# A longer assumed delay between dependent steps in the list scheduler of a fused graph convolution and expert network, while edge tiles are left

## The chip, the core and the metric

One core of a Trainium2 chip runs the kernel as one program. It has five instruction queues that run each in their own order and meet only at semaphores: TensorE (PE), VectorE (DVE), ScalarE (ACT), GpSimd (POOL) and SyncE (SP, which here only issues DMAs). The metric is the device time of the program in microseconds (us), lower is better.

## What is computed

Cut to what matters (6,250 nodes, 106,250 edges, width 256; 8 experts of hidden width 1,024, the best two per node):

```python
z   = layernorm(x) @ W * norm_src                  # per node
h   = segment_sum(z[src], dst) * norm_dst + b      # gather by edge, sum by target node
x   = x + relu(h)
n   = layernorm(x)
top_p, top_idx = top_k(softmax(layernorm(n) @ Wr + br), 2)
y_e = gelu(xe @ W1[e] + b1[e]) @ W2[e] + b2[e]     # for the two experts of each node
out = x + sum(weights * y_e)
```

The layer norm of the second network has a gain and a shift per expert, and W is applied behind the sum.

## The kernel before

**Edges.** The edges, sorted by target, are cut in 832 edge tiles of 128 edges. For each tile POOL gathers 128 rows of the table `zt` with one indirect DMA (L830) into one of 23 buffers `gt` (a gather waits until the tile 22 places earlier has been used), and PE multiplies them by a 0/1 matrix `S` (L1159, step `tile`). Eight tiles make a run, which DVE adds to the sums in `acc` (L1528, step `add`).

**Node tiles.** The 49 tiles of 128 nodes lie in 15 groups and 8 chunks. As soon as the edges of a group are summed, each node tile runs through the steps `nT` (PE transposes, ACT copies), `nW` (product with W on PE), `hh` (DVE: relu, residual, statistics), `xT` (transpose again) and `lg` (router logits on PE). `nd1` and `nd2` are DVE work per group ahead and behind. When a chunk is whole, `r1`, `r3`, `r5`, `r6` compute the routing, and POOL sends its rows by expert to DRAM (`xs`, L858, two indirect DMAs for each node tile: a **send**).

**Blocks.** A block is 256 rows of one expert; there are 56, and a chunk's blocks can start when its rows are sent. SP loads the rows and weights (`ld`: rows `xb` L1018, `w1b` L1022; `ld2`: `w2b` L1028, bias L1032). Then `turn` (PE transposes L1229, ACT copies), `low` (DVE, L1650, the lower halves `xe`), four `up` steps (PE, 12 products each, L1245; ACT computes the gelu L1106 and a copy L1110), a `split` on DVE behind each (L1656), two `down` steps (PE, 24 products each, L1260) and `y` on DVE (L1682). The loads of `w1b` for block m wait until the four `up` of block m-2 are done.

**Results.** Blocks 0 to 33 hold rows of the chunks 0 to 5. Their results are stored to a table `ys` in DRAM by SP (`st`, L985). When all edge tiles and all of these stores are done, POOL **fetches them back** for the 41 node tiles of these chunks (`cg`, L877, two DMAs each); DVE adds the two rows of each node with their weights (`cc`, L1695 and L1696), and four sums (`sums`, L899) add the outcome to `out`. The blocks 34 to 55 add theirs to `out` by an indirect DMA with addition, two for each block (a **give**, L890). Gives and sums form one chain: each waits until the one ahead of it has landed. Four of these 22 blocks are of chunk 6, and 18 (38 to 55) of chunk 7, the last, whose sends need the last edge tile.

**Order.** A scheduler, `plan()`, writes one list of steps in Python when the program is built, and each engine takes its own part of that list in the list's order. `plan()` keeps a clock of its own for each engine, and lets a step be listed when what it depends on is done by that clock. The end of a step, as its dependents see it, is what `emit` returns: the costs, and `HAND` = 0.5 on top.

Of the kernel before, what the change touches and what calls it, by code (L numbers as in the profile page):

```python
# [159 lines left out]
PARTS = {"wa": ("w", "wb"), "wc": ("w", "wd"), "we": ("w", "wf"), "nW": ("n", "hh"), "r3": ("r", "r5")}  # L160


ROUTE = {f"r{i}": i for i in range(10)}


def plan():
# [4 lines left out]
    later, sent = [], {}  # L171

    turns, used = [], set()
    HAND, SLACK = 0.5, 0.5

    BEHIND = [1.25 * min(8, (R * CT - 1 - i) // 2) for i in range(R * CT)]

    def emit(kind, arg, costs, ready):
        order.append((kind, arg))
        t = ready  # L180
        for eng, us in costs:
            t = max(t, clock[eng]) + us
            clock[eng] = t
            t += 0.2
        return t + HAND

    def free(costs):
        return all(clock[eng] <= s["now"] + (3.0 if i else 1.0) for i, (eng, _) in enumerate(costs) if eng != "POOL")
# [1 line left out]
    def due():  # L190

        done = False
        while later and later[0][0] <= s["now"]:
            at, kind, arg, costs, then = later.pop(0)
            end = emit(kind, arg, costs, at)
            then(end)
            done = True
        return done
# [6 lines left out]
    def blocks():  # L205
# [12 lines left out]
        def turn(m):  # L218
            end = emit("turn", m, (("PE", 0.55), ("ACT", 0.65)), s["now"])
            after(end, "low", m, (("DVE", 0.75),), lambda e: low.__setitem__(m, e))  # L220

        def up(m, q):
            end = emit("up", (m, q), (("PE", 1.35), ("ACT", 1.85)), s["now"])
            after(end, "split", (m, q), (("DVE", 0.8),), lambda e: split.__setitem__((m, q), e))
# [183 lines left out]
    n = R * CT  # L408
    at = {"g": 0, "fetch": 0, "tile": 0}
# [46 lines left out]
def gnn_ffn(nc, x, src, dst, W, b, Wr, br, ln_g, ln_b, W1, b1, W2, b2, out):  # L456
# [3 lines left out]
    ACT = mybir.ActivationFunctionType  # L460
    X = mybir.AxisListType.X
    ORDER = plan()

    ctx = ExitStack()
    with ctx:
# [798 lines left out]
        def vector(e):  # L1264
            made = {"n": 0}

            def then(inst):

                made["n"] += 1
                inst.then_inc(s_chain, 1)  # L1270
                e.wait_ge(s_chain, made["n"])
# [242 lines left out]
            for kind, arg in ORDER:  # L1514
# [112 lines left out]
                elif kind == "lr":  # L1627
# [7 lines left out]
                    then(e.tensor_tensor(lg[:, js, :], lg[:, js, :], br_bc[:, :].unsqueeze(1).to_broadcast([128, n, E]), ALU.add))  # L1635
                elif kind in ROUTE:
                    route(arg, ROUTE[kind])
                elif kind == "turn":
# [88 lines left out]
```

## Time and profile before

| | us |
|---|---|
| median of 3 runs | 1662.88 |
| lowest and highest | 1661.35, 1666.77 |
| span of the profiled execution | 1657.8 |
| PE busy | 1196.1 |
| POOL busy | 1122.3 |
| DVE busy | 951.9 |
| ACT busy | 595.5 |

The median of the runs is 5.1 us above the profiled execution's span; this much is taken for what lies around the span. The trace knows three stages. Up to about 160 us the tables are made. Then the gathers run, up to about 1336 us, with node tiles and blocks in between. Behind them lies the end stage, with the last chunk, the fetches back, the last blocks and the gives. In a row of a timeline the first number is the start from the start of the span, the second the duration, and the bracket the idle time ahead of it on its engine with what ended it.

### The profile page before, as it was taken

The numbers are of one execution on the slowest core, as the hardware profiler recorded it, in microseconds if no ns is written. First come the engines' busy times: TensorE is split into PE (matmuls) and PEld (weight loads), VectorE is DVE, ScalarE is ACT, GpSimd is POOL, SyncE is SP. The second block draws the span as 40 slices with busy tenths as digits, with TensorE's granted clock in tenths as the row PEclk, the third lists the DMA queues.
The fourth block names the chain that finished last, engine by engine and source line by source line (L and its number), as shares of the span: only waits on it lengthen the run. The fifth ranks groups of instructions, "written<-read, shape, count | busy, mean of one in ns | idle before, by whom it ended". The sixth has DMA issues, their size and how long they took to land.

```text
span 1657.8 us, 26613 instructions
## 1 busy us (share of the span) xinstructions
PE 1196.1 (72%) x9098; PEld 988.4 (60%) x9098; DVE 951.9 (57%) x2502; ACT 595.5 (36%) x1169; POOL 1122.3 (68%) x1116
## 2 busy tenths in 40 slices
PE   6954556756358555995499649969848868688996
PEld 5954344535147224983388439848728746577995
DVE  8997457556435252657264744764645639465543
ACT  4954011111032003540345125515315335355663
POOL 5006777777777777777777777777777757864333
PEclk9999566557579557996799769979959969899998
DMA  6027866776485348974787569869659578999983
GB/s 187 1 97 264 270 218 214 220 230 180 129 261 163 110 117 262 293 241 130 251 283 246 144 202 320 272 193 300 188 185 307 171 239 240 279 305 289 255 243 93
DMA packets 262266, 356.06 MB, mean 215 GB/s; under 512 B 25476, under 2 KB 225702, under 8 KB 262132
## 3 DMA queue, kind: packets, MB, share of 16 engines
q1 hardware_dynamic: 195544, 205.39, 38.4%
q0 software_dynamic: 60224, 142.57, 30.1%
q10 hardware_dynamic: 6364, 6.40, 1.2%
q8 instruction: 73, 1.20, 0.3%
q14 instruction: 61, 0.50, 0.1%
HBM read 290.80 MB, written 65.38 MB: 215 GB/s over the span
## 4 chain that ended last, share of the span: by engine, by line
PE 36%; DMA 23%; POOL 18%; issue 9%; DVE 9%; ACT 3%; SPq 1%; POOLq 0%; DVEq 0%; ACTq 0%
DMA gt<-zt,srcI 12%; PE ps L1245 9%; PE ps L1260 9%; POOL gt L830 9%; PE ps L1159 8%; POOL xs L858 5%; DMA out<-gt,toks 4%; PE ps L1134 2%; PE ps L1170 2%; DVE ohl L1334 2%; PE ps L1197 2%; POOL out L890 2%; ACT h L1106 2%; POOL S L877 1%; DMA out<-acc 1%
## 5 line engine op out<-in xcount | busy, mean ns | idle before, releaser
L830 POOL DMA_INDIRECT gt<-zt,srcI x832 | 832.8, 1001 | 254.2 <-issue 180.1
L1159 PE MATMUL ps<-gt,S 128*128 128x257 f16 x1664 | 346.9, 332 | 199.6 <-DMA gt<-zt,srcI 198.4
L1159 PEld LDWEIGHTS ps<-gt,S 128*128 128x128 f16 x1664 | 202.9, 152 | 298.9 <-DMA gt<-zt,srcI 283.2
L1245 PE MATMUL ps<-xe,w1b 128*128 128x256 f16 x2688 | 345.5, 283 | 40.7 <-DVE xe L1650 19.9
L1260 PE MATMUL ps<-w2b,hT 128*128 128x256 f16 x2688 | 313.3, 274 | 13.4 <-DVE yb L1682 6.8
L1245 PEld LDWEIGHTS ps<-xe,w1b 128*128 128x128 f16 x2688 | 270.3, 101 | 85.3 <-DVE xe L1650 22.6
L1106 ACT ACTIVATE h<-ps,cb 128x256 f32<-128x256 f32 x448 | 227.5, 558 | 251.4 <-PE ps L1245 250.2
L1656 DVE SCALAR_TENSOR_TENSOR hT<-h,cb,hT 128x512 f16<-128x512 f32 x224 | 167.5, 749 | 235.1 <-ACT hT L1110 234.5
L1260 PEld LDWEIGHTS ps<-w2b,hT 128*128 128x128 f16 x2688 | 263.4, 98 | 46.9 <-issue 12.8
L1110 ACT ACTIVATE hT<-h,cb 128x512 f16<-128x512 f32 x224 | 161.7, 722 | 7.3
L1084 ACT ACTIVATE aT<-ps 128x256 f32<-128x256 f32 x98 | 37.5, 382 | 316.4 <-PE ps L1190 316.3
L1382 DVE TENSOR_TENSOR S<-dlo,S 128x1024 f16<-128x1024 f16 x104 | 71.7, 690 | 103.1 <-PE ps L1159 102.4
L890 POOL DMA_INDIRECT out<-gt,toks x38 | 63.0, 1657 | 94.6 <-DMA out<-gt,toks 52.7
L858 POOL DMA_INDIRECT xs<-xrow,slI x98 | 98.4, 1004 | 31.9 <-issue 29.6
L1094 ACT ACTIVATE xe<-ps 128x512 f16<-128x512 f32 x56 | 32.5, 580 | 238.6 <-PE ps L1229 238.6
L1229 PE MATMUL ps<-ident,xb 128*128 128x128 f32 x224 | 37.8, 296 | 102.1 <-DMA xb<-xs 102.1
L1650 DVE SCALAR_TENSOR_TENSOR xe<-ps,xe 128x512 f16<-128x512 f32 x56 | 38.3, 683 | 118.0 <-ACT xe L1094 118.0
L1528 DVE SCALAR_TENSOR_TENSOR acc<-ps,dhi,acc 128x257 f32 x208 | 91.1, 479 | 22.9 <-PE ps L1159 10.6
L1229 PEld LDWEIGHTS ps<-ident,xb 128*128 128x128 f32 x224 | 28.3, 152 | 105.6 <-DMA xb<-xs 104.8
L1134 PE MATMUL ps<-ohh,ohl 128*128 128x49 bf16 x832 | 84.1, 278 | 9.8 <-DVE ohh L1335 9.2
L1134 PEld LDWEIGHTS ps<-ohh,ohl 128*128 128x128 bf16 x832 | 81.2, 150 | 12.9 <-DVE ohh L1335 12.9
L1170 PE MATMUL ps<-gb,w1b 128*128 128x1 f32 x256 | 51.9, 337 | 34.4 <-DMA w1b<-in_L_ffn_W 34.4
(261 smaller groups left out, 1253.0 us busy)
## 6 DMA issues: line engine op xcount, KB each, us to landing
w1b<-ws SPq DMA_DIRECT2D x56, 1024.0 KB, 6.6
w2b<-ws SPq DMA_DIRECT2D x56, 1024.0 KB, 9.2
ws<-w2b SPq DMA_DIRECT2D x16, 1024.0 KB, 5.3
xb<-xs SPq DMA_DIRECT2D x56, 260.0 KB, 8.0
gt<-zt,srcI POOLq DMA_INDIRECT x832, 3.8
ys<-yb SPq DMA_DIRECT2D x34, 256.0 KB, 7.4
w1b<-in_L_ffn_W SPq DMA_DIRECT2D x8, 1024.0 KB, 9.2
hT<-in_L_ffn_W SPq DMA_DIRECT2D x8, 1024.0 KB, 13.6
```

The lines of the kernel that those rows point to most:

```text
L830: e.indirect_dma_start(out=gt[:, i % NG, :], out_offset=None, in_=zt, in_offset=bass.IndirectOffsetOnAxis(ap=srcI[:, c, r:r + 1].bitcast(u ...
L858: e.indirect_dma_start(out=xs, out_offset=bass.IndirectOffsetOnAxis(ap=slI[:, i, CHUNKS[c][0] + j:CHUNKS[c][0] + j + 1].bitcast(u32), axis=0),
L890: e.indirect_dma_start(out=out, out_offset=bass.IndirectOffsetOnAxis(ap=toks[:, a, i:i + 1].bitcast(u32), axis=0), in_=late_rows(a)[:, i, ...
L1106: inst = e.activation(h32[n % NH][:, z, :], UP[n % 2][:, z * BS:(z + 1) * BS], ACT.Gelu, bias=cb[m % 3][:, 2 * q + z:2 * q + z + 1], scale ...
L1110: e.activation(hT[m % 2][:, 0, 2 * q:2 * q + 2, :], h32[n % NH][:, :, :], ACT.Copy, scale=cb[m % 3][:, 9:10]).then_inc(s_hi, 1)
L1134: inst = e.matmul(PS[6][:, 0:T], ohl[c % 2][:, :, j], ohh[c % 2][:, :, j], start=(c == 0 and j == 0), stop=(c == NCH - 1 and j == TC - 1))
L1159: inst = e.matmul(PS[r % 2][:, 0:257], S[:, r % NS, :, c], gt[:, i % NG, part * 257:part * 257 + 257], start=(c == 0 and part == 0), stop= ...
L1170: inst = e.matmul(PV[:, j:j + 1], w3[:, kk, j * 128:(j + 1) * 128], gb[:, ex, 2 + kk:3 + kk], start=(kk == 0), stop=(kk == 1))
L1245: inst = e.matmul(UP[n % 2][:, z * BS:(z + 1) * BS], w[:, l, kk, j * 128:(j + 1) * 128], xe[m % 2][:, k, kk, :], start=(kk == 0 and l == 0 ...
L1260: inst = e.matmul(PY[:, h * D:(h + 1) * D], hT[m % 2][:, k, j, h * 128:(h + 1) * 128], w[:, l, j, :], start=(j == 0 and l == 0 and k == 0) ...
L1528: inst = e.scalar_tensor_tensor(out=a, in0=PS[r % 2][:, 0:257], scalar=dhi[:, w, r:r + 1], in1=a, op0=ALU.mult, op1=ALU.add)
L1656: e.scalar_tensor_tensor(out=hT[m % 2][:, 1, 2 * q:2 * q + 2, :], in0=h32[n % NH][:, :, :], scalar=cb[m % 3][:, 9:10], in1=hT[m % 2][:, 0, ...
```

## The change

`emit` adds 2.5 in place of 0.5 behind the steps `turn`, `low`, `up`, `split`, `down`, `nT`, `nW`, `hh` and `xT`, as long as the list has not yet come to the last edge tile (`at["tile"] < n`, n = 832). No instruction is added or taken away (3,360 steps in both lists); the steps change their places.

```diff
@@ -160,6 +160,9 @@
+SPREAD = ("turn", "low", "up", "split", "down", "nT", "nW", "hh", "xT")
@@ -171,7 +174,7 @@
-    HAND, SLACK = 0.5, 0.5
+    HAND, SLACK, FAR_HAND = 0.5, 0.5, 2.5
@@ -182,7 +185,7 @@
-        return t + HAND
+        return t + (FAR_HAND if kind in SPREAD and at["tile"] < n else HAND)
```

In the list of before, the `y` of block 30 stands behind edge tile 785, that of block 33 behind tile 824, and block 34 is the next when the edge tiles end. In the list of the change the `y` of block 30 stands behind tile 813, and behind the last edge tile come the last `up` of block 32, half of block 31's `down`, all of block 32's, and the whole of block 33 from its first `up` on. Lines behind the new constants are three higher.

**First place: the end of the gathers.** On PE, from the last edge tile on: L1190 and L1193 are the transposes of node tiles, L1197 and L1200 the product with W, L1206 and L1209 the logits, L1245 and L1248 `up`, L1260 and L1263 `down`, L1229 and L1232 `turn`. Before:

```order
L1159 MATMUL ps<-gt,S 128x257 x8
L1190 MATMUL ps<-ident,acc 128x128 x4
L1245 MATMUL ps<-xe,w1b 128x256 x12
L1197 MATMUL ps<-W_sb,aT 128x256 x2
L1190 MATMUL ps<-ident,acc 128x128 x2
L1245 MATMUL ps<-xe,w1b 128x256 x24
L1229 MATMUL ps<-ident,xb 128x128 x4
L1197 MATMUL ps<-W_sb,aT 128x256 x2
L1190 MATMUL ps<-ident,acc 128x128 x2
L1245 MATMUL ps<-xe,w1b 128x256 x12
L1206 MATMUL ps<-Wrc,aT 128x8 x2
L1197 MATMUL ps<-W_sb,aT 128x256 x2
```

With the change:

```order
L1162 MATMUL ps<-gt,S 128x257 x2
L1193 MATMUL ps<-ident,acc 128x128 x4
L1248 MATMUL ps<-xe,w1b 128x256 x12
L1263 MATMUL ps<-w2b,hT 128x256 x24
L1200 MATMUL ps<-W_sb,aT 128x256 x2
L1193 MATMUL ps<-ident,acc 128x128 x2
L1248 MATMUL ps<-xe,w1b 128x256 x24
L1200 MATMUL ps<-W_sb,aT 128x256 x2
L1193 MATMUL ps<-ident,acc 128x128 x2
L1263 MATMUL ps<-w2b,hT 128x256 x24
L1209 MATMUL ps<-Wrc,aT 128x8 x2
L1248 MATMUL ps<-xe,w1b 128x256 x24
```

Before, the first products are those of block 34; now those of the blocks 32, 31 and 33 stand ahead of it, and `down` steps lie between the steps of the node tiles.

On POOL, at the same place: L830 and L833 are gathers, L858 and L861 sends (8 DMAs for chunk 6, then 8 for chunk 7), L877 and L880 fetches back, L890 and L893 gives, L899 and L902 the first sum. Before:

```order
L830 DMA gt<-zt,srcI 128x514 x71
L858 DMA xs<-xrow,slI 53504x260 x8
L830 DMA gt<-zt,srcI 128x514 x7
L877 DMA S<-ys,cidx 128x256 x8
L877 DMA gt<-ys,cidx 128x256 x6
L877 DMA xrow<-ys,cidx 128x256 x6
L877 DMA S<-ys,cidx 128x256 x6
L890 DMA out<-yb,toks 6250x256 x2
L877 DMA S<-ys,cidx 128x256 x2
L877 DMA gt<-ys,cidx 128x256 x4
L899 DMA out<-acc 128x10x256
L858 DMA xs<-xrow,slI 53504x260 x8
```

With the change:

```order
L833 DMA gt<-zt,srcI 128x514 x68
L861 DMA xs<-xrow,slI 53504x260 x8
L880 DMA S<-ys,cidx 128x256 x8
L880 DMA gt<-ys,cidx 128x256 x6
L861 DMA xs<-xrow,slI 53504x260 x8
L893 DMA out<-yb,toks 6250x256 x2
L880 DMA xrow<-ys,cidx 128x256 x6
L880 DMA S<-ys,cidx 128x256 x4
L893 DMA out<-yb,toks 6250x256 x2
L880 DMA S<-ys,cidx 128x256 x4
L880 DMA gt<-ys,cidx 128x256 x2
```

The sends of chunk 6 moved behind the last gather. The sends of chunk 7 moved ahead of the first give and of most fetches back: 14 fetch DMAs stand ahead of them, and 32 did before.

**Second place: SP around the store of block 33** (with buffer numbers; L985 and L988 are the store `ys<-yb0`, L1018 and L1021 a block's rows, L1022 and L1025 its `w1b`). Before:

```order
L1032 DMA b2b0<-in_L0_ffn_b2 128x256
L1018 ISA
L1018 DMA xb3<-xs 128x2x260
L1022 ISA
L1022 DMA w1b1<-ws0 128x8x512
L985 DMA ys<-yb0 128x2x256
L938 DMA xin<-in_x 106x256
```

With the change:

```order
L948 TENSOR_LOAD ek6
L948 ISA x2
L1021 ISA
L1021 DMA xb0<-xs 128x2x260
L1025 ISA
L1025 DMA w1b0<-ws0 128x8x512
L988 DMA ys<-yb0 128x2x256
L1031 DMA w2b1<-ws1 128x8x512
```

Before, the store stands behind `w1b1` of block 35; now behind `w1b0` of block 36.

**Third place: DVE at the first block of chunk 7.** L1646 and L1649 are the DVE part of `turn` of block 38, L1650 and L1653 its `low`, L1695 to L1699 `cc`, with the buffer that the fetched rows lie in. Before:

```order
L1695 TENSOR_SCALAR acc<-gt,wts 128x256
L1696 SCALAR_TENSOR_TENSOR acc<-gt,wts,acc 128x256
L1642 TENSOR_LOAD ek
L1642 ISA x2
L1646 ISA
L1646 COPY cb<-cbt 128x12
L1695 TENSOR_SCALAR acc<-xrow,wts 128x256
L1696 SCALAR_TENSOR_TENSOR acc<-xrow,wts,acc 128x256
L1650 SCALAR_TENSOR_TENSOR xe<-ps,xe 128x512
```

With the change:

```order
L1698 TENSOR_SCALAR acc<-S,wts 128x256
L1699 SCALAR_TENSOR_TENSOR acc<-S,wts,acc 128x256
L1645 TENSOR_LOAD ek
L1645 ISA x2
L1649 ISA
L1649 COPY cb<-cbt 128x12
L1698 TENSOR_SCALAR acc<-S,wts 128x256
L1699 SCALAR_TENSOR_TENSOR acc<-S,wts,acc 128x256
L1698 TENSOR_SCALAR acc<-gt,wts 128x256
L1699 SCALAR_TENSOR_TENSOR acc<-gt,wts,acc 128x256
L1653 SCALAR_TENSOR_TENSOR xe<-ps,xe 128x512
```

Ahead of this `low` stood the `cc` of node tile 17 with that of 16 ahead of it; now it is those of the tiles 12, 13 and 14, which the new list of POOL fetches behind the sends of chunk 7 and behind two gives.

## Rows read from the trace of the kernel before

**Rows 1.** The profile's page: span, busy time and share of each engine.

```profile
span 1657.8 us, 26613 instructions
...
PE 1196.1 (72%) x9098; PEld 988.4 (60%) x9098; DVE 951.9 (57%) x2502; ACT 595.5 (36%) x1169; POOL 1122.3 (68%) x1116
```

**Rows 2.** Waits of POOL, 161 to 1338 us: releaser: us in total, times, longest.

```profile
POOL gt L830 <- issue: 173.4, 569, 0.3
POOL gt L830 <- PE ps L1159: 73.7, 242, 0.3
POOL xs L858 <- issue: 27.4, 90, 0.3
```

**Rows 3.** Waits of PE, 400 to 1340 us, same columns.

```profile
PE ps L1229 <- DMA xb<-xs: 98.2, 7, 28.1
...
PE ps L1190 <- ACT aT L1084: 11.2, 15, 1.6
```

**Rows 4.** Timeline of POOL: start, us, operation [idle before it <-releaser].

```profile
1317.89 1.02 POOL L858 DMA_INDIRECT xs<-xrow,slI  x1 [0.30 <-issue]
...
1328.27 0.99 POOL L830 DMA_INDIRECT gt<-zt,srcI  x1 [0.30 <-issue]
...
1335.83 0.95 POOL L830 DMA_INDIRECT gt<-zt,srcI  x1 [0.30 <-issue]
1347.60 0.94 POOL L877 DMA_INDIRECT S<-ys,cidx  x1 [10.81 <-DMA ys<-yb]
1348.85 0.94 POOL L877 DMA_INDIRECT S<-ys,cidx  x1 [0.30 <-issue]
```

**Rows 5.** Timeline of PE, same columns: last edge tile, blocks 37, 38 and 55.

```profile
1342.59 0.65 PE L1159 MATMUL ps<-gt,S 128*128 128x257 f16 x2 [1.10 <-DMA gt<-zt,srcI]
...
1397.47 2.78 PE L1245 MATMUL ps<-xe,w1b 128*128 128x256 f16 x24
1400.09 2.78 PE L1260 MATMUL ps<-w2b,hT 128*128 128x256 f16 x24
...
1423.74 6.66 PE L1245 MATMUL ps<-xe,w1b 128*128 128x256 f16 x36 [3.51 <-DVE xe L1650]
...
1639.63 5.40 PE L1260 MATMUL ps<-w2b,hT 128*128 128x256 f16 x48 [1.70 <-DVE gt L1682]
```

**Rows 6.** Timeline of SP's DMA issues; then issues by line, us to landing last.

```profile
1334.47 3.81 SPq L985 DMA_DIRECT2D ys<-yb  x1
...
ys<-yb SPq DMA_DIRECT2D x34, 256.0 KB, 7.4
```

**Rows 7.** Timeline of DVE: last node tile, its group, a fetched row.

```profile
1372.75 0.18 DVE L1605 BATCH_NORM_AGGREGATE mv<-st 128x2 f32<-128x6 f32 x1
...
1375.59 0.17 DVE L1281 SCALAR_TENSOR_TENSOR ra<-tm,ra 128x8 f32<-128x8 f32 x1
...
1422.21 0.35 DVE L1695 TENSOR_SCALAR acc<-xrow,wts 128x256 f32<-128x256 f32 x1 [4.16 <-DMA xrow<-ys,cidx]
```

**Rows 8.** Timeline of POOL after the edges: a send, fetches back, gives.

```profile
1397.60 1.07 POOL L858 DMA_INDIRECT xs<-xrow,slI  x1 [2.30 <-DVE slI L1445]
...
1408.27 1.59 POOL L890 DMA_INDIRECT out<-yb,toks  x1 [0.30 <-issue]
...
1412.05 1.04 POOL L877 DMA_INDIRECT gt<-ys,cidx  x1 [0.30 <-DVE acc L1696]
...
1415.93 0.95 POOL L877 DMA_INDIRECT xrow<-ys,cidx  x1 [0.30 <-DMA out<-yb,toks]
...
1546.90 1.66 POOL L890 DMA_INDIRECT out<-gt,toks  x1 [12.14 <-DMA out<-acc]
...
1636.95 1.55 POOL L890 DMA_INDIRECT out<-gt,toks  x1 [7.69 <-DMA out<-gt,toks]
...
1647.83 1.55 POOL L890 DMA_INDIRECT out<-gt,toks  x1 [2.06 <-DMA out<-gt,toks]
```

**Rows 9.** Waits of PE, 1424 to 1646 us, columns as in Rows 2.

```profile
PE ps L1245 <- DVE xe L1650: 14.5, 6, 3.5
```

## The prediction

> **What bounds the kernel now.** I read the page first: in a span of 1657.8 us PE is busy for 1196.1 and POOL for 1122.3 [rows 1], and no engine is full. Such shares hide that the program has two stages with different limits, so I ask each stage which wait ends last.
>
> *While gathers run* (161 to 1338 us): the waits of POOL [rows 2] show that no gather and no send waited longer than 0.3 us. The 0.3 us is the normal step between two DMAs, so POOL issues one about each 1.25 to 1.3 us from first to last, and its own issue sets the pace. PE waits for the gathers, and much for the first rows of a chunk: 98.2 us in 7 waits, the longest 28.1 [rows 3]. Even behind that one POOL did not wait, since 23 buffers lie between them. The waits of PE for other engines' results, which the change wants to lessen, are small: the largest kind is 11.2 us, for ACT's copies [rows 3]. Nothing that PE saves here can pull a gather forward.
>
> *Behind the gathers*: the last gather starts at 1335.83, the last edge tile ends at 1342.59 + 0.65 = 1343.24 [rows 4, 5]. POOL then waits 10.8 us for the store of block 33 and starts the fetches back at 1347.60 [rows 4]. From there it works almost without a gap, and then from give to give: 1546.90 to 1636.95 are 10 gives, 9.0 us each, each held by the landing of the one ahead; the last two come 5.4 us apart [rows 8], when PE has ended or nearly so and loads no more weights. PE runs the 18 blocks of chunk 7 from 1423.74 and ends at about 1645 [rows 5]; the last give starts at 1647.83 [rows 8]. So two chains end together. The one of POOL has been behind its inputs since the sums, and I take it as the bound: what delays the first fetch back, delays the end.
>
> **The change part by part.** Up to the last gather the counts are the same, and POOL sets the pace, so the new places cost nothing there; the cover is the 23 buffers, and it would be gone if PE fell 22 tiles behind (27 us at 1.25).
>
> *Sends of chunk 6 behind the last gather.* Eight DMAs of (1328.27 - 1317.89) / 8 = 1.30 us leave the path of the gathers [rows 4]: the last gather starts at 1325.4, the last edge tile ends at 1343.2 - 10.4 = 1332.8. A gain of 10.4 for all that hangs on that tile.
>
> *Blocks pushed behind the last edge tile.* By the order of PE these are one quarter of the `up` of block 32, half of block 31's `down`, all of 32's, and block 33 whole. In units of 24 products of 2.62 us (1400.09 - 1397.47 [rows 5]): 0.5 + 1 + 2 + 4 = 7.5 units, 19.7 us of PE.
>
> *When block 33 is stored.* Its `y` now follows, on DVE, the statistics of the last node tile and the end of that group. Before, these statistics ended at 1372.93, 29.7 us behind the last edge tile, and the group's end took 2.8 more [rows 7]. PE has 6.5 units in that stretch where it had 4; I assume they fit, and price it at 2.5 x 2.62 = 6.5 us if not. So `y` ends at 1332.8 + 29.7 + 2.8 + 0.8 = 1366. Its store stands on SP behind the weights of block 36, which wait for the four `up` of block 34, and PE comes to these only behind block 33: 1362 for the last `down`, then 2 units with the node steps in between and a `turn`: 1369 to 1371. I take 1371. The store landed in 7.4 us at the median and in about 13 the last time (1334.47 to 1347.60 [rows 4, 6]), then behind much more queued weight data; I take 10. The fetches back start at **1381**, 33.4 us later than before. Bounds: 1369 + 7.4 = 1376 (+29), and 1371 + 6.5 + 13 = 1391 (+43).
>
> The Trainium skill ("DMA: Bandwidth & Descriptors", section "Anatomy of one DMA — SWDGE (gpsimd) path") gives about 2.0 us fixed plus bytes over 436 GB/s: as an estimate 2.6 us for these 256 KB, and the sum would be 7.4 us less by it. It states this for GpSimd's DMAs, this one is SP's, and the row of 7.4 speaks against it; the row decides.
>
> *From the first fetch back to the gives.* 82 fetches, 8 sends, 9 gives and 4 sums stand there in both orders, so I keep before's distance to the give at 1546.90, less the 2.3 us that POOL waited for the slots of chunk 7 [rows 8], which are now known before POOL asks. So this give starts at 1546.9 + 33.4 - 2.3 = 1578.
>
> *When chunk 7's blocks start.* Its sends now stand behind 14 fetches, but the `low` of block 38 stands on DVE behind the `cc` of node tile 14. Ahead of that tile's second row lie 29 fetches of 1.25 (1348.85 - 1347.60 [rows 4]), 8 sends of 1.3 and two gives of 3.8 (1412.05 - 1408.27 [rows 8]): 1381 + 36.3 + 10.4 + 7.6 = 1435.3. The fetch that held this `low` before was issued at 1415.93 [rows 8], and DVE took it up at 1422.21 after a wait of 4.16 [rows 7]: 6.3 us. With `cc` and `low`, 1.5 us, `up` starts at 1443 instead of 1423.74: PE is 19 us later, POOL's chain 31.
>
> *Sum.* PE ends 12 us earlier against the chain than before, so 12 / 9.0 = 1.3 gives more run at 5.4 and not at 9.0: -4.8. 33.4 - 2.3 - 4.8 = **+26.3 us**, span 1684.1. With the 5.1 us by which the median stands above the span: **1689 us**. Bounds: 29 - 2.3 - 4.8 = +22 and 43 - 2.3 - 4.8 = +36; half a microsecond more or less for each of 10 gives adds 5 at both ends: 1680 to 1704.
>
> **Rivals.** *PE alone sets the end.* If the gives catch up on the late fetches (POOL is idle for over half of each 9 us), only PE's work counts: 19.7 more, 10.4 earlier, +9.3 at most, and less where the work falls in PE's idle time there: 1663 to 1672. For it: PE and gives end within 3 us of each other. Against: each give waited for the one ahead, long after its own block was done, and `cc` 14 holds PE too.
>
> *Faster: chunk 7 sets the end.* Its path starts at the last edge tile, which comes 10.4 us earlier; if all behind it moves along, 1662.9 - 10.4 = 1652.5. For it: the 10.4 us are sure. It decides at the fetches: the sends were at 1397.60 [rows 8] and would have to be at 1387.2, so the 14 fetches (17.8 us) would have to start by 1369.4, where I have 1381 and 1376 at the earliest.
>
> The rule of the Trainium skill that speaks for a gain is "Perfetto Trace Analysis", section "Optimization Strategies": keep the matmul engine as busy as possible and unblock what it waits for. By it the waits of 11.2 us in [rows 3] would come off the end; that POOL never waited says they would not.
>
> *More: DVE's order makes every block wait.* If each of the ten blocks up to the last `cc` waits 3.5 us for fetched rows, the longest such wait now, PE gets 35 us where 14.5 of the kind are in its present run [rows 9]: its end is 1645 + 19 + 20.5 = 1684.5, and with the 12.8 us from there to the span's end 1697.3: time 1702. It decides when PE ends after about 1679.
>
> *Nothing*: the list changes nothing that binds. The order of POOL and SP speaks against it; it is in the lower end of the PE rival.
>
> **Chances.** The forecast 0.67; PE alone 0.14 (half of it within 0.3% of now); faster 0.06; every block waits 0.11; none of these 0.02. A measurement of this kernel can tell about 0.3%, 5 us, from no change. Faster 0.07, same 0.07, slower 0.86. The range takes in the bounds of the sum and most of both rivals at its sides: 1672 to 1706.
>
> **What would show it.** Right: the last gather starts near 1325 with no wait of POOL above 0.3 us ahead of it; then POOL idle for 30 to 45 us until a store `ys<-yb`; the first `up` of block 38 near 1443 behind a DVE wait for fetched rows; gives about 9 us apart, the last four or so 5.4. Wrong: POOL waits for PE among the gathers; fetches back that start before 1370; gives held by DVE's `y` and not by the one ahead, which would be PE's bound; a node chain of over 36 us behind the last edge tile.

## The result, and the profile after

| | before | after |
|---|---|---|
| median, us | 1663.66 (4 runs) | 1683.45 (4 runs) |
| lowest and highest, us | 1661.35, 1666.77 | 1679.6, 1685.85 |
| span of the profiled execution, us | 1657.8 | 1684.4 |

The change makes the kernel slower: the ratio after to before is 1.0126, with a 95% interval of 1.0094 to 1.0157. The forecast was 1689, with a range from 1672 to 1706.

The page of the kernel after, first part, answers to [rows 1]. The share of PE even rises by a point while the time gets longer:

```profile
span 1684.4 us, 26608 instructions
...
PE 1224.4 (73%) x9098; PEld 1011.4 (60%) x9098; DVE 948.6 (56%) x2502; ACT 596.5 (35%) x1169; POOL 1125.2 (67%) x1116
```

**While gathers run.** Waits of POOL from 161 to 1325 us (releaser: us in total, times, longest), beside [rows 2]:

```profile
POOL gt L833 <- issue: 178.8, 587, 0.3
POOL gt L833 <- PE ps L1162: 66.7, 219, 0.3
POOL xs L861 <- issue: 25.0, 82, 0.3
```

As before, no gather waited longer than 0.3 us. And the waits of PE in this stage (400 to 1330 us), beside [rows 3]:

```profile
PE ps L1162 <- DMA gt<-zt,srcI: 151.0, 165, 3.8
PE ps L1232 <- DMA xb<-xs: 71.1, 4, 23.7
...
PE ps L1193 <- ACT aT L1087: 9.9, 16, 1.9
```

The wait for ACT's copies, which room between dependent steps should lessen, went from 11.2 to 9.9 us. The wait for the rows of chunks fell by 27 us, from 98.2 to 71.1, and that for the gathers rose by 33.5, from 117.5 to 151.0: what PE saves at one it waits at the other.

**Behind the gathers.** Timeline of POOL, beside [rows 4, 8]: the last gather, the first and last send of chunk 6, the first fetch back, the first send of chunk 7, the first give, the give behind the last sum, the last.

```profile
1328.72 1.07 POOL L833 DMA_INDIRECT gt<-zt,srcI  x1 [0.30 <-PE ps L1162]
1331.49 1.02 POOL L861 DMA_INDIRECT xs<-xrow,slI  x1 [1.70 <-DVE slI L1448]
...
1340.56 0.98 POOL L861 DMA_INDIRECT xs<-xrow,slI  x1 [0.30 <-issue]
1381.14 0.99 POOL L880 DMA_INDIRECT S<-ys,cidx  x1 [39.59 <-DMA ys<-yb]
...
1399.10 1.02 POOL L861 DMA_INDIRECT xs<-xrow,slI  x1 [0.30 <-issue]
...
1410.61 1.61 POOL L893 DMA_INDIRECT out<-yb,toks  x1 [0.30 <-issue]
...
1581.77 1.67 POOL L893 DMA_INDIRECT out<-gt,toks  x1 [15.27 <-DMA out<-acc]
...
1674.25 1.56 POOL L893 DMA_INDIRECT out<-gt,toks  x1 [2.06 <-DMA out<-gt,toks]
```

The one large new thing is the idle time of 39.6 us ahead of the first fetch back, where 10.8 stood. Everything behind it on POOL moved with it: the first fetch back by 33.5 us, the give behind the last sum by 34.9, the last give by 26.4, the span by 26.6.

The timeline of SP shows what the fetch waited for, beside [rows 6]: rows and weights of block 36, then the store of block 33, which stands behind them in the list.

```profile
1368.53 0.39 SPq L1021 DMA_DIRECT2D xb<-xs  x1
1373.62 0.39 SPq L1025 DMA_DIRECT2D w1b<-ws  x1
1374.06 0.58 SPq L988 DMA_DIRECT2D ys<-yb  x1
```

DVE, beside [rows 7]: the statistics of the last node tile, then `y` of block 33, ready 5.3 us before its store is issued. Those 5.3 us are a queue's order, and no work.

```profile
1365.11 0.18 DVE L1608 BATCH_NORM_AGGREGATE mv<-st 128x2 f32<-128x6 f32 x1
...
1367.97 0.75 DVE L1685 SCALAR_TENSOR_TENSOR yb<-ps,cb,b2b 128x512 f32<-128x512 f32 x1
```

PE, beside [rows 5]: the last edge tile, the first `up` of block 38, the last `down`.

```profile
1334.01 0.64 PE L1162 MATMUL ps<-gt,S 128*128 128x257 f16 x2
...
1446.75 4.22 PE L1248 MATMUL ps<-xe,w1b 128*128 128x256 f16 x36 [2.41 <-DVE xe L1653]
...
1651.90 5.40 PE L1263 MATMUL ps<-w2b,hT 128*128 128x256 f16 x48 [1.72 <-DVE gt L1685]
```

PE ends at 1657.3, 17 us ahead of the last give; before, it was 2.8 us.

### The profile page after: what moved, and what is told of

It is laid out like the page before. It is cut to its first block, busy times and chain, and to the rows that moved or that the text cites. A ratio compares the mean times of both kernels' runs of the same rounds, so it can differ in the third digit from the quotient of the medians.

```text
span 1684.4 us, 26608 instructions
## 1 busy us (share of the span) xinstructions
PE 1224.4 (73%) x9098; PEld 1011.4 (60%) x9098; DVE 948.6 (56%) x2502; ACT 596.5 (35%) x1169; POOL 1125.2 (67%) x1116
## 4 chain that ended last, share of the span: by engine, by line
PE 32%; DMA 29%; POOL 21%; issue 10%; DVE 7%; ACT 1%; POOLq 0%; DVEq 0%; SPq 0%; ACTq 0%
DMA gt<-zt,srcI 20%; POOL gt L833 11%; PE ps L1162 8%; PE ps L1263 8%; PE ps L1248 8%; POOL xs L861 5%; DMA out<-gt,toks 4%; PE ps L1137 2%; PE ps L1173 2%; DVE ohl L1337 2%; DMA out<-acc 2%; POOL out L893 2%; PE ps L1200 2%; DVE zh L1351 1%; POOL S L880 1%
## 5 line engine op out<-in xcount | busy, mean ns | idle before, releaser
L833 POOL DMA_INDIRECT gt<-zt,srcI x832 | 834.5, 1003 | 254.1 <-issue 185.8
L1248 PE MATMUL ps<-xe,w1b 128*128 128x256 f16 x2688 | 353.4, 287 | 17.6 <-DVE xe L1653 15.0
L1263 PE MATMUL ps<-w2b,hT 128*128 128x256 f16 x2688 | 323.2, 279 | 17.7 <-DVE yb L1685 13.8
L1248 PEld LDWEIGHTS ps<-xe,w1b 128*128 128x128 f16 x2688 | 276.3, 103 | 62.8 <-DVE xe L1653 19.0
L1263 PEld LDWEIGHTS ps<-w2b,hT 128*128 128x128 f16 x2688 | 268.5, 100 | 55.7 <-issue 17.6
L861 POOL DMA_INDIRECT xs<-xrow,slI x98 | 100.9, 1029 | 31.3 <-issue 29.6
L893 POOL DMA_INDIRECT out<-gt,toks x38 | 60.4, 1589 | 86.4 <-DMA out<-gt,toks 43.1
L1531 DVE SCALAR_TENSOR_TENSOR acc<-ps,dhi,acc 128x257 f32 x208 | 91.0, 479 | 29.1 <-PE ps L1162 12.2
L1232 PE MATMUL ps<-ident,xb 128*128 128x128 f32 x224 | 36.9, 291 | 71.1 <-DMA xb<-xs 71.1
L1173 PEld LDWEIGHTS ps<-gb,w1b 128*128 128x128 f32 x256 | 53.2, 321 | 34.7 <-issue 34.5
L1232 PEld LDWEIGHTS ps<-ident,xb 128*128 128x128 f32 x224 | 28.3, 151 | 72.8 <-DMA xb<-xs 72.0
```

The costliest lines, as they stand in the source:

```text
L833: e.indirect_dma_start(out=gt[:, i % NG, :], out_offset=None, in_=zt, in_offset=bass.IndirectOffsetOnAxis(ap=srcI[:, c, r:r + 1].bitcast(u ...
L861: e.indirect_dma_start(out=xs, out_offset=bass.IndirectOffsetOnAxis(ap=slI[:, i, CHUNKS[c][0] + j:CHUNKS[c][0] + j + 1].bitcast(u32), axis=0),
L893: e.indirect_dma_start(out=out, out_offset=bass.IndirectOffsetOnAxis(ap=toks[:, a, i:i + 1].bitcast(u32), axis=0), in_=late_rows(a)[:, i, ...
L1173: inst = e.matmul(PV[:, j:j + 1], w3[:, kk, j * 128:(j + 1) * 128], gb[:, ex, 2 + kk:3 + kk], start=(kk == 0), stop=(kk == 1))
L1248: inst = e.matmul(UP[n % 2][:, z * BS:(z + 1) * BS], w[:, l, kk, j * 128:(j + 1) * 128], xe[m % 2][:, k, kk, :], start=(kk == 0 and l == 0 ...
L1263: inst = e.matmul(PY[:, h * D:(h + 1) * D], hT[m % 2][:, k, j, h * 128:(h + 1) * 128], w[:, l, j, :], start=(j == 0 and l == 0 and k == 0) ...
```

## The experiments

In what follows "first fetch" is the start of the first fetch back, "last give" the start of the first DMA of the last block's give. In every kernel the span ends about 10 us after that start. The executions behind a profile vary by some us around their median, so the medians decide and the profile tells the place.

### On which stretch does it hang: spreading up to the end, or at the end alone

Theory A: the cost comes from what is pushed behind the last edge tile, so nearly all of it from the last 130 edge tiles. Its rival: the new order costs (or gains) within the gathers. Four kernels test it, each an edit of the kernel after. e1 ends the spreading 130 tiles before the end:

```diff
-        return t + (FAR_HAND if kind in SPREAD and at["tile"] < n else HAND)
+        return t + (FAR_HAND if kind in SPREAD and at["tile"] < n - 130 else HAND)
```

e2 spreads only there:

```diff
-        return t + (FAR_HAND if kind in SPREAD and at["tile"] < n else HAND)
+        return t + (FAR_HAND if kind in SPREAD and n - 130 <= at["tile"] < n else HAND)
```

e3 spreads only the steps of blocks, e4 only those of node tiles:

```diff
-SPREAD = ("turn", "low", "up", "split", "down", "nT", "nW", "hh", "xT")
+SPREAD = ("turn", "low", "up", "split", "down")
```

```diff
-SPREAD = ("turn", "low", "up", "split", "down", "nT", "nW", "hh", "xT")
+SPREAD = ("nT", "nW", "hh", "xT")
```

Expected of e1:

> The change, with the longer assumed delay given up once edge tile 702 is listed, 130 ahead of the end. Theory (the late fetches back carry the loss): block 33's result is listed ahead of the last edge tile again, its store is not behind the weights of block 36, the first fetch back starts at 1345 to 1352, and the time is that of the kernel before, 1658 to 1668. Rival (spreading costs through the gather stage itself): most of the stage is still spread, so at least half of the loss stays, 1673 or more.

Expected of e2:

> The reverse: the longer assumed delay is used only from edge tile 702 to the last. Three of the ten block steps behind the last edge tile are gone against the full change (all of block 33's down, half of its up and half of block 32's down twice remain), and the store stands ahead of block 36's weights. Theory: the first fetch back starts between 1360 and 1374, 7 to 20 us ahead of the full change, and the time is 1668 to 1678, between the two kernels. Rival (the spread of the gather stage costs): 1658 to 1667, as before the change.

Expected of e3:

> The longer delay for the steps of blocks alone (turn, low, up, split, down). Three down steps of the blocks 32 and 33 stand behind the last edge tile, the sends of chunk 6 are back among the gathers, so the last edge tile is 10 us later than with the full change. Theory: the first fetch back at 1363 to 1373, time 1669 to 1678. If PE's added work alone counted: 3 x 2.6 = 8 us of work, time 1664 to 1671.

Expected of e4:

> The longer delay for the steps of node tiles alone (nT, nW, hh, xT). The same three down steps stand behind the last edge tile, but the sends of chunk 6 come behind the last gather, which ends 10 us earlier. Theory: the first fetch back at 1353 to 1365, time 1661 to 1671. If PE's added work alone counted: 8 us of work less the 10 us head start, time 1657 to 1664.

Beside these four the kernel before itself took 1900.08 us (1888.6 to 1913.8), 14% more than in every other measurement of this document. Why is not known: the record gives the same chip number, 7, for these and for the later e1 again, beside which the kernel before took 1661.24 us. The times that the four expectations name can't be compared with these, only the ratios can:

| | us | ratio to before | interval |
|---|---|---|---|
| e1, no spreading at the end | 1934.22 | 1.0179 | 1.0139 to 1.0219 |
| e2, only at the end | 1914.87 | 1.0078 | 1.0051 to 1.0106 |
| e3, blocks only | 1933.61 | 1.0166 | 1.0113 to 1.022 |
| e4, node steps only | 1918.91 | 1.01 | 1.0066 to 1.0135 |

The waits of POOL in e1 (161 to 1500 us) show another regime than [rows 2]:

```profile
POOL gt L833 <- issue: 198.3, 631, 3.1
POOL gt L833 <- PE ps L1162: 125.2, 100, 10.5
POOL gt L833 <- remote: 73.5, 53, 4.9
```

Here gathers do wait for PE, up to 10.5 us at a time, and for things that the trace names only as "remote". In those moments the 23 buffers no longer covered PE. The traces of the four let one see where e1 lost more than e2: its last gather starts at 1562.81 and not at 1533.04 (some 10 us of this are the sends of chunk 6, which stand among its gathers), yet its first fetch is earlier, at 1585.28 and not at 1589.74. Its first give then waits 23.8 us for the result of its block, and its last give comes 19.2 us later than that of e2 (1920.22 and 1900.99):

```profile
1644.30 1.63 POOL L893 DMA_INDIRECT out<-yb,toks  x1 [23.77 <-DVE yb L1691]
```

So in this regime the start of the first fetch does not order the kernels, and blocks that are late on PE do reach the gives. By the ratios the spreading before the last 130 tiles costs most there; between steps of blocks (e3) and of node tiles (e4) the intervals overlap. No trace of the kernel before was taken in this regime, so how much of the waiting is the change's own is open. The four decide nothing about the case's own time, and e1 and e2 were run again. (The list of e2 has six of the ten block steps behind the last edge tile, so four are gone, and not three as its expectation says.)

> The kernel of the run e1_no_spread_at_end once more, beside kernels of this call. Theory: the time of the kernel before, within 0.3% of it. Rival (spreading costs through the gather stage itself): 10 us or more above the kernel before.

> The kernel of the run e2_spread_only_at_end once more, beside kernels of this call: the longer assumed delay only from edge tile 702 on. Theory: the first give of the end stage starts between the kernel before (1381.7) and the change (1410.6), the time is 1668 to 1678. Rival (spreading through the gather stage costs): within 0.3% of the kernel before.

Measured, where the kernel before takes its usual time:

| | us | before, us | ratio | first fetch | last give |
|---|---|---|---|---|---|
| before | | | 1 | 1347.6 | 1647.8 |
| e1 again | 1667.9 | 1661.24 | 1.0033 (1.0014 to 1.0053) | 1352.7 | 1656.6 |
| e2 again | 1674.5 | 1660.27 | 1.0082 (1.0055 to 1.011) | 1368.1 | 1668.7 |
| after | 1683.45 | 1663.66 | 1.0126 (1.0094 to 1.0157) | 1381.1 | 1674.3 |

Waits of POOL at the first fetch back, in e1 again and then in e2 again:

```profile
1352.68 0.94 POOL L880 DMA_INDIRECT S<-ys,cidx  x1 [13.72 <-DMA ys<-yb]
```

```profile
1368.10 0.99 POOL L880 DMA_INDIRECT S<-ys,cidx  x1 [18.02 <-DMA ys<-yb]
```

In e2 again POOL also stands 12.3 us ahead of the first send of chunk 6, between the last gather and this wait.

Here the order of the two is turned round: most of the cost comes from the last 130 tiles. It is not all of it: e1 again misses both of its forecasts, since it costs 0.33% (more than nothing, by its interval) and not 10 us. Spreading before the last 130 tiles leaves 5.1 us of delay at the first fetch. The two parts (0.33 and 0.82%) add to 1.15, within the interval of the whole. The cost grows with the start of the first fetch in all four kernels, as Theory A says; but the PE work behind the last edge tile grows along with it (no, six and ten block steps), so these runs alone do not part the two. How much blocks and node steps contribute at the usual time was not run.

### Is it the store behind the weights

e5 keeps the list of the kernel after, and moves one step: the store of block 33 to a place right behind its `y`, ahead of the loads of block 36.

```diff
+    order.remove(("st", M0 - 1))
+    order.insert(order.index(("y", M0 - 1)) + 1, ("st", M0 - 1))
```

> The changed kernel, with one step moved: the store of block 33 stands on SP right behind the end of the last group, ahead of the rows and weights of block 36, so that it no longer waits for the up steps of block 34. In the trace of the change block 33's y ended at 1368.7 and the store was issued at 1374.1, so it can go 5 us earlier, and 1 MB of weights is no longer queued ahead of it. Theory (the first fetch back sets the end): it starts 5 to 8 us earlier than with the change, and the time is 4 to 8 us below the change's, 1675 to 1680. Rival (PE's work alone sets the end): no change, 1683.

Measured: 1676.74 us, ratio 1.0094 (1.0062 to 1.0125). The store on SP, the first fetch and the last give:

```profile
1363.37 0.37 SPq L990 DMA_DIRECT2D ys<-yb  x1
```

```profile
1368.98 1.00 POOL L882 DMA_INDIRECT S<-ys,cidx  x1 [27.58 <-DMA ys<-yb]
...
1664.41 1.56 POOL L895 DMA_INDIRECT out<-gt,toks  x1 [2.06 <-DMA out<-gt,toks]
```

The store is issued at the end of its `y` (1362.59 + 0.75 on DVE), the first fetch starts 12.2 us earlier and the last give 9.8. Not all of the 12.2 is the edit's: 5.3 us are the wait of the store for its place, 1.5 its quicker landing, and 5.4 come from a `y` that was earlier in this execution. The medians give 6.7 us against the kernel after, within the 4 to 8 of the theory, the ratios 0.3%, and the intervals of the two ratios overlap; e9 below, measured beside e5 with the store in its late place, took 6.9 us more than e5. PE's work is the same in kind and place. So one step's place on SP is worth a quarter to a third of the loss. The rest of the wait, 27.6 us, lies ahead of the end of `y`: PE works through the pushed blocks and the last node tiles almost without a gap, and the last `down` of block 33 ended at 1366.2 in the kernel after, 31.5 us behind the last edge tile.

### Does the first block of chunk 7, held by DVE's order, set the end

e9 is the kernel after with `cc` of the node tiles 10 to 14 put behind the `low` of block 38 on DVE, so that this block need not wait for fetched rows.

```diff
+    held = [("cc", t) for t in range(10, 15)]
+    order[:] = [step for step in order if step not in held]
+    after_low = order.index(("low", M0 + NBLK[LAST - 1])) + 1
+    order[after_low:after_low] = held
```

> The changed kernel, with DVE's combination of the fetched rows of node tiles 10 to 14 moved behind the low of block 38. PE no longer waits for the fetches 12 to 14, and the up steps of block 38 should start 8 to 15 us earlier (1446.75 with the change), as its rows land near 1428. The fetches and gives on POOL keep their places. Theory (POOL's chain of gives sets the end): PE ends 8 to 15 us earlier, at most one or two more gives run without load, and the time is 0 to 6 us below the change's. Rival (PE sets the end): the time falls by the whole 8 to 15 us.

Measured: 1683.67 us, ratio 1.0126 (1.0084 to 1.0168), the ratio of the kernel after to the last digit. The `up` of block 38 starts 13.2 us earlier than in the kernel after, as expected, but the block behind it then waits for its `low`; PE ends 3.8 us earlier, the last give at the same time:

```profile
1433.56 4.21 PE L1252 MATMUL ps<-xe,w1b 128*128 128x256 f16 x36
...
1446.04 4.90 PE L1252 MATMUL ps<-xe,w1b 128*128 128x256 f16 x24 [6.52 <-DVE xe L1657]
...
1648.06 5.40 PE L1267 MATMUL ps<-w2b,hT 128*128 128x256 f16 x48 [1.70 <-DVE gt L1689]
```

```profile
1377.00 0.99 POOL L884 DMA_INDIRECT S<-ys,cidx  x1 [34.48 <-DMA ys<-yb]
...
1674.12 1.56 POOL L897 DMA_INDIRECT out<-gt,toks  x1 [2.06 <-DMA out<-gt,toks]
```

This execution's first fetch was 4.1 us earlier by itself, which is as much as PE's whole gain. So the run shows that block 38's wait for fetched rows costs nothing at the end. Since PE's end hardly moved, it does not show what an earlier end of PE would be worth.

### The other side: the kernel before with an early store

If the first fetch sets the time, the kernel before should gain from a store that is never late. e8 takes the list of before, holds the sends of chunk 6 until the last gather is out (the 10.4 us that the change gained), and puts the store of block 33 right behind its `y`.

```diff
+                if kind == "xs" and arg[0] == LAST - 1 and at["fetch"] < n:
+                    continue
...
+    order.remove(("st", M0 - 1))
+    order.insert(order.index(("y", M0 - 1)) + 1, ("st", M0 - 1))
```

> The kernel before, with block 33 stored as soon as its y is listed (ahead of the loads of block 34) and the sends of chunk 6 held back until the last gather is listed. This undoes the late store and keeps what the change gained. Theory: the gathers end 10 us earlier, the first fetch back starts at 1336 to 1341 behind the sends instead of 1347.6, and both chains start 7 to 10 us earlier: 1652 to 1658. Rival (the end is set by PE's work and blocks 34 to 37 cannot start before their rows land): 1661 to 1668.

Measured: 1658.7 us, ratio 0.9984 (0.9962 to 1.0005). No wait is left between the last gather and the fetches:

```profile
1325.48 0.95 POOL L834 DMA_INDIRECT gt<-zt,srcI  x1 [0.30 <-issue]
...
1337.09 0.99 POOL L881 DMA_INDIRECT S<-ys,cidx  x1 [0.30 <-issue]
```

and yet PE ends much earlier and the last give hardly:

```profile
1625.91 5.40 PE L1264 MATMUL ps<-w2b,hT 128*128 128x256 f16 x48 [1.70 <-DVE gt L1686]
```

```profile
1646.49 1.56 POOL L894 DMA_INDIRECT out<-gt,toks  x1 [2.06 <-DMA out<-gt,toks]
```

The time lies between the two forecasts (1652 to 1658, and 1661 to 1668). The first fetch is 10.5 us earlier, PE ends 13.7 us earlier, and the time moves by 0.2%, less than can be told from nothing. So PE's work does not set the end here, and neither does the first fetch alone. Where the head start goes can be seen at the first give, before and then in e8:

```profile
1381.66 1.83 POOL L890 DMA_INDIRECT out<-yb,toks  x1 [0.30 <-issue]
```

```profile
1384.15 1.83 POOL L894 DMA_INDIRECT out<-yb,toks  x1 [0.30 <-issue]
```

It starts 2.5 us later than before and not earlier. The list of e8 has 28 fetches and the 8 sends of chunk 7 ahead of the first give, that of before 26 fetches; this takes 47.1 us from the first fetch where it took 34.1. So POOL had used up the head start before the chain of gives and sums began, and e8 tests an earlier first fetch, not an earlier chain. From the first give to the last it took 262.3 us and before 266.2. Within the chain e8 waits more for landings. Before, from 1333 to 1690 us:

```profile
POOL out L890 <- DMA out<-gt,toks: 52.7, 11, 7.7
POOL out L890 <- DMA out<-acc: 20.4, 2, 12.1
POOL out L890 <- issue: 18.4, 30, 6.2
```

and e8, same stretch:

```profile
POOL out L894 <- DMA out<-gt,toks: 58.4, 13, 6.5
POOL out L894 <- DMA out<-acc: 34.5, 4, 15.5
...
POOL out L894 <- issue: 7.9, 26, 0.3
```

The waits for the landings of gives and of sums rise by 5.7 + 14.1 us. Those named "issue" fall by 10.5, though: before, a wait of 6.2 us behind a sum stands under that name, so part of the rise is only a better name for the same kind of wait. Over the executions of all kernels the first give and the last are 259.0 to 268.2 us apart, but for e10 and for e11, whose chain begins with a sum; from the first fetch to the last give it is 293 to 314 us.

### What in the chain of POOL takes up a head start

Three kernels ask this. e6 is e8 with a delay on POOL ahead of the first give, twelve fills of an unused tile (7.2 us and their waits):

```diff
+                    if last is None:
+                        for z in range(LAGS):
+                            e.memset(lag[:, :], 0.0).then_inc(s_gen, 1)
+                            e.wait_ge(s_gen, z + 1)
```

> The kernel of e8_before_early_store with 12 fills of an unused tile on POOL ahead of the first give, some 8 to 12 us in which POOL issues nothing. In e8 PE ended at 1631.3 and the last give started at 1646.5, so PE is some 12 us ahead of the gives. Theory, as the runs so far sharpen it (the chain of 22 gives and 4 sums takes 262 to 268 us from its first give to its last in every kernel, so the start of the first give sets the end): the time rises by the lag, 8 to 12 us above e8. Rival (PE's blocks set the end): PE is late by less than the room of 12 us, and the time rises by 0 to 3 us.

Measured: 1663.97 us, ratio 1.0015 (0.9993 to 1.0037).

```profile
1387.20 7.19 POOL L896 MEMSET lag<- 128x512 f32 x12
1395.20 1.62 POOL L902 DMA_INDIRECT out<-yb,toks  x1 [0.80 <-POOL lag L896]
...
1654.20 1.56 POOL L902 DMA_INDIRECT out<-gt,toks  x1 [2.06 <-DMA out<-gt,toks]
```

The first give is 11.05 us later than in e8 (1384.15); 3.3 of that is the later first fetch of this execution (1340.37), the rest the fills. At the last give 7.7 of the 11.05 are left (e8: 1646.49), and by the medians 5.3 us (each ran beside a kernel before of its own, and these differ by 1.0). Theory had 8 to 12 us and its rival 0 to 3, so neither came. Of the 11.05 us at the first give, half (by the medians) to 0.7 (by the traces) come out at the end. PE's end was later too, by 8.3 us, of which the later start of this execution may be some 3, though no step of PE was delayed by the edit.

e10 is the kernel after with the first give moved ahead of the sends of chunk 7, to start the chain of gives earlier:

```diff
+    first = ("give", M0)
+    order.remove(first)
+    order.insert(order.index(("xs", (LAST, 0))), first)
```

> The changed kernel with the first give moved on POOL ahead of the sends of chunk 7. Nothing on PE moves. In the trace of the change block 34's result was ready at 1399.9, the sends took POOL from 1399.1 to 1410.3, and the give started at 1410.6. Now it can start at 1400, and the sends and the fetches come 4 us later. Theory (the first give's start sets the end): the last give is 8 to 10 us earlier, time 1673 to 1677. Rival (the first fetch back, or PE, sets the end): the same time as the change or up to 4 us more, 1682 to 1688.

Measured: 1682.69 us (1677.41 to 1687.22), ratio 1.0143 (1.0093 to 1.0193). In the execution profiled:

```profile
1372.47 0.99 POOL L883 DMA_INDIRECT S<-ys,cidx  x1 [35.13 <-DMA ys<-yb]
...
1391.66 1.72 POOL L896 DMA_INDIRECT out<-yb,toks  x1 [1.31 <-DVE yb L1694]
...
1419.61 1.62 POOL L896 DMA_INDIRECT out<-yb,toks  x1 [0.30 <-issue]
...
1665.80 1.56 POOL L896 DMA_INDIRECT out<-gt,toks  x1 [2.06 <-DMA out<-gt,toks]
```

The time is that of the rival. The first give starts 19 us earlier (8.7 of this is this execution's earlier first fetch), but the second waits for nothing and still starts only at 1419.61: POOL is busy with sends and fetches up to there. First fetch to last give is 293.3 us, as in the kernel after (293.1), although first give to last give grew from 263.6 to 274.1. This speaks for POOL's whole stretch as what counts, not the start of the chain of gives; since it is one pair of executions and the interval is wide, a gain of some us from the earlier give is not excluded.

e11 is e8 with the first sum ahead of the sends of chunk 7, and the `cc` of the node tiles 7 to 9 moved up so that this is possible:

```diff
+    early_cc = [("cc", t) for t in range(7, SUMS[0][1])]
+    order[:] = [step for step in order if step not in early_cc]
+    behind = order.index(("cc", 6)) + 1
+    order[behind:behind] = early_cc
+    order.remove(("sums", 0))
+    order.insert(order.index(("xs", (LAST, 0))), ("sums", 0))
```

> The kernel of e8_before_early_store with the first sum moved ahead of the sends of chunk 7, and the combination of the node tiles 7 to 9 ahead of block 35's first split. The chain of gives and sums then starts with a sum at about 1373 in place of a give at 1384. Theory (the chain's start sets the end): the sum lands near 1389, the first give is 5 us later than in e8 and the chain has one long link of 14 to 17 us fewer behind it: 8 to 12 us less than e8, 1645 to 1652, until PE's own end (1631 in e8, here some us later) binds. Rival (PE's blocks set the end): no gain over e8.

Measured: 1659.71 us, ratio 1.0006 (0.9983 to 1.0029): a miss, the gain did not come, as the rival had it. The sum and the give behind it run well, and the next sum waits:

```profile
1373.31 1.87 POOL L909 DMA_DIRECT2D out<-acc  x1
...
1387.26 1.57 POOL L900 DMA_INDIRECT out<-yb,toks  x1 [1.35 <-DMA out<-acc]
...
1426.93 1.83 POOL L909 DMA_DIRECT2D out<-acc  x1 [9.20 <-DVE acc L1706]
```

POOL stands 9.2 us still at the second sum until DVE has done its `cc`. The head start of a link is lost at the next place where two orders meet. None of the kernels beats the kernel before by more than its measurement can tell; e8 is the nearest, at 0.9984.

## Why the prediction was right, and where it was not

**The bound while gathers run: right.** No wait of POOL above 0.3 us up to the last gather. The runs beside a kernel before of 1900 us show the other case: there gathers waited for PE up to 10.5 us at a time. (By the code a gather waits for the tile 23 places earlier, not 22; nothing hangs on it.)

**The gain of 10.4 us at the last edge tile: mis-sized.** The last gather started at 1328.72, not 1325.4; the tile ended at 1334.65, not 1332.8, a gain of 8.6. POOL waited no more than before, but its gathers were busy for 834.5 us where it had been 832.8, which is 1.7 of the 3.3 us, and the 82 sends that still lie among them took 1.02 us each where it had been 1.00, which is the other 1.7.

**The start of the first fetch back: right to 0.1 us, by two errors that cancel.** `y` ended at 1368.7, not at 1366 (1.9 of this is the late edge tile; the last `down` ended at 1366.2, not at 1362), and the weights of block 36 went out at 1373.62, so the store was issued at 1374.06 and not at 1371. Against this, it landed in about 7 us (1374.06 to 1381.14), where I had taken 10 between the median of 7.4 and 13 from before. Nearly the same lists gave 1377.00 and 1372.47 in the profiled executions of e9 and e10, so that precision was luck in any case. That the place of the store counts is shown by e5: the step moved alone gave 6.7 us against the kernel after by the medians and 0.3% by the ratios. For the other two thirds the late fetch and PE's extra work come together, and no run parts them.

**From the first fetch to the give behind the last sum: near.** 1578 was predicted, it started at 1581.77: the distance grew by 1.3 us instead of falling by 2.3. The wait for the slots did go (0.30 and not 2.30 at the first send of chunk 7), but the give behind the last sum waited 15.3 us for it and not 12.1.

**The rest of the chain of gives: mis-sized.** From there to the last give it took 92.5 us, where it had been 100.9 before. That is a gain of 8.4, and I had priced 4.8 by the number of gives that run when PE has ended. PE ended 17 us ahead of the last give, not 12 + 2.8 = 15, and the gives stood 5.4 to 11.1 us apart, two of them at 6.5 (ended by the gives at 1606.48 and 1642.38) well before PE's end. The misses of this and of the step before cancel, 3.6 against 3.6.

**The first block of chunk 7: right in kind.** Its `up` started at 1446.75 behind a `low` held by `cc`, where 1443 was forecast. PE ended at 1657.3, 6.7 us before the 1664 of my sum, since it then waited only 11.8 us where it had waited 21. The wait of this block cost nothing, as e9 shows, where its `up` started 13.2 us earlier at the same time of the whole.

**From the spans to the medians: 5.5 us too high.** The sum itself came out between the two profiled executions: their spans differ by 26.6 us, my sum said 26.3. But each run's time is only 1.5 us above its own span (1685.85 and 1684.4, 1679.6 and 1678.1, and so on), so the execution profiled before took 1659.3, 4.4 below its median of now, and the one after took 1685.85, 2.4 above. Without these 6.8 us the change costs 19.8, the difference of the medians. I had added 5.1 us to a span as what lies around it; 1.5 of that was so, and 3.6 was a quick execution. Whether too large a share of the delay was let through to the end can't be told apart from this: the interval of the ratio, 0.94 to 1.57%, is 16 to 26 us, and the two later kernels with nearly the same list (e9, e10) cost 22.4 us each by their medians. In this pair of traces 0.8 of the delay at the first fetch reached the last give (26.4 of 33.5), which is what the sum had allowed; against the same trace of before it was 0.8 in e5 and 1.0 in e2 again. The store, the term on which all hangs, was forecast well only by the two errors named above.

**The rivals.** *PE alone sets the end*: its time, 1663 to 1672, did not come, and e8 speaks against it, where PE ended 13.7 us earlier for nothing. It had a grain of truth in that not all of the delay reaches the end. Over the kernels, 33.5 us at the first fetch (of the profiled execution) gave 19.8 us by the medians, 21.4 gave 15.5 (e5), 20.5 gave 14.2 (e2 again), 5.1 gave 6.7 (e1 again), and 10.5 earlier gave 2.5 (e8). That is 0.6 to 0.7 of each us for the large delays; since executions of nearly one list had first fetches up to 8.7 us apart, these shares are rough. *Chunk 7 sets the end*: fell, its sends stood at 1399.10 and not by 1387.2; in e8 they start at 1373.30, and nothing measurable is gained. *Every block waits for DVE*: did not come; of such waits only 5.8 us were left on PE from 1447 on. *Nothing*: excluded by the interval.

**What stays open.** What takes up a part of a delay in POOL's stretch, and how large that part is: from nothing to a fifth by the traces with a late fetch, 0.3 to 0.4 by the medians. Which point of POOL's stretch counts: the first give moved alone brought nothing that can be told (e10). PE ends earlier against the chain in the kernel after and the last gives are then quicker (17 us against 2.8), but no run tested it alone, and none delayed PE alone. Nor was it tried whether blocks or node steps push more work behind the last edge tile at the usual time, nor why the kernel before once took 1900 us.

## What to carry to other kernels

An assumed delay in a list scheduler acts on every queue that shares the list: it smoothed waits of PE that cost nothing, and pushed a store behind weight loads on SP, where it held the queue whose stretch is longest. After such a change, look first at what moved past the end of the stage whose bound is about to change hands, and at each step that another queue's whole remaining stretch waits for. And where two chains seem to end together, delay one and then the other. Here half or more of a delay on POOL came out at the end, and 14 us saved on PE did not; a delay of PE alone is the run that is missing. When a head start comes to nothing, look for the first place where it is gone: in e8 it was gone at the first give, ahead of every wait that the totals point at.

## What the runs showed of the hardware

- One program can run 14% longer (1900.08 us against 1660 to 1664), though the record names the same chip, 7, for one of the usual measurements. The granted clock was 0.79 to 0.81 there and 0.81 to 0.84 in the others. Gathers then waited up to 10.5 us for PE, and two variants that cost 0.33 and 0.82% at the usual time cost 1.8 and 0.8%. The mean gather itself took no longer (1,002 ns in e1 and 1,001 in e1 again).
- The same store of 256 KB landed in 5.6 us (e5) and 7.1 us (after), and in about 13 before, where the DMAs of more weights had been issued ahead of it.
- With nearly equal lists up to that point, the first fetch back started between 1372.5 and 1381.1 us in three executions. A single pair of profiles can thus be off by as much as the whole forecast error.
